# One layer norm for two, later rounding of two batches and ScalarE's own loads, at the start of a gated cross-attention kernel

## The reference

```python
m = jnp.mean(x, axis=axis, keepdims=True)
v = jnp.var(x, axis=axis, keepdims=True)
return (x - m) / jnp.sqrt(v + eps)                     # _layernorm, eps 1e-5
...
return (x - mu) * jax.lax.rsqrt(var + EPS) * w + b     # _ln of the result, EPS 1e-5
...
y = jnp.clip(x.astype(jnp.float32) / scale, -FP8_MAX, FP8_MAX)
y = y.astype(jnp.bfloat16).astype(jnp.float32)
return _fp8_roundtrip(y)                               # _div_clamp_fp8
```

## Time and profile before

| what | value |
|---|---|
| runs | 820.71, 820.9, 822.23 us, median 820.9 |
| the profiled execution's own time | 819.82 us |
| its span in the profile | 818.0 us |
| PE, DVE, ACT, POOL busy | 89%, 75%, 57%, 56% of the span |

### The profile page before, as it was taken

How to read it: one execution, slowest core, us unless ns; L and a number is a source line. 1 busy time by engine, 2 the same in 40 slices (tenths; PEclk the granted TensorE clock), 3 DMA queues, 4 the chain that set the end, 5 groups by cost and what they waited for, 6 DMA issues and landing times.

```text
span 818.0 us, 15329 instructions
## 1 busy us (share of the span) xinstructions
PE 726.0 (89%) x4859; PEld 589.4 (72%) x4859; DVE 613.4 (75%) x1290; ACT 466.6 (57%) x1178; POOL 459.7 (56%) x592
## 2 busy tenths in 40 slices
PE   2548999899999989999998999998886886999996
PEld 2546787778788778878787878887664654777775
DVE  6867888788888878889887898987876592444554
ACT  3656867677676767867667686775652231222221
POOL 3464777566777756777775767776673213222220
PEclk9779999999999999999999999999999596999999
DMA  5320000100010010001001010000020103666661
GB/s 181 97 64 1 27 27 1 52 27 27 1 40 15 1 53 26 26 7 48 1 1 53 1 33 27 1 3 0 1 60 0 64 2 110 191 187 189 199 192 53
DMA packets 44478, 42.74 MB, mean 52 GB/s; under 512 B 3717, under 2 KB 43386, under 8 KB 44410
## 3 DMA queue, kind: packets, MB, share of 16 engines
q1 hardware_dynamic: 42874, 36.62, 14.8%
q0 software_dynamic: 1536, 5.28, 2.4%
HBM read 39.52 MB, written 2.37 MB: 51 GB/s over the span
## 4 chain that ended last, share of the span: by engine, by line
PE 62%; DVE 20%; issue 6%; ACT 5%; POOL 4%; SPq 2%; DMA 1%; POOLq 0%; DVEq 0%; ACTq 0%
PE out_ps L1718 8%; PE proj_ps L1458 7%; PE s_ps L1502 6%; PE proj_ps L1443 5%; PE pT_ps L1511 5%; PE aux_ps L1521 5%; PE aux_ps L1535 5%; DVE q_tok L1086 5%; PE aux_ps L1472 4%; PE proj_ps L1434 4%; PE work_ps L1710 3%; POOL rstd L527 3%; PE work_ps L1732 2%; DVE ss L1066 2%; DVE pT_sb L1111 2%
## 5 line engine op out<-in xcount | busy, mean ns | idle before, releaser
L542 POOL TENSOR_SCALAR p_sb<-p_sb,psum_row 128x256 f32<-128x256 f32 x256 | 125.8, 507 | 69.0 <-DVE psum_row L1105 67.7
L796 ACT ACTIVATE p_sb<-s_ps,negmax 128x256 f32<-128x256 f32 x256 | 118.5, 473 | 66.3 <-DVE negmax L1100 65.2
L1521 PE MATMUL aux_ps<-pT_sb,v_sb 128*128 128x512 f32 x256 | 122.3, 601 | 6.1 <-DVE pT_sb L1111 6.1
L1111 DVE COPY pT_sb<-pT_ps 128x512 f32<-128x512 f32 x128 | 87.7, 686 | 47.5 <-PE pT_ps L1511 46.8
L1502 PE MATMUL s_ps<-kT,qT 128*128 128x256 f32 x768 | 112.7, 289 | 8.2 <-DVE qT L1096 4.6
L549 POOL TENSOR_TENSOR y_bf<-y_bf,mg_bf 128x512 bf16<-128x512 bf16 x64 | 86.0, 1343 | 58.5 <-DVE mg_bf L1123 58.5
L1502 PEld LDWEIGHTS s_ps<-kT,qT 128*128 128x128 f32 x768 | 98.0, 190 | 18.3 <-issue 18.3
L1100 DVE TENSOR_REDUCE negmax<-s_ps 128x2 f32<-128x512 f32 x128 | 86.5, 683 | 5.9 <-PE s_ps L1502 5.6
L527 POOL TENSOR_TENSOR rstd<-var,minus_half 128x8 f32<-128x8 f32 (+1 forms) x64 | 86.6, 1354 | 5.5 <-POOL var L523 0.4
L552 POOL TENSOR_TENSOR catq<-y_bf,mg_bf 128x512 fp32r<-128x512 bf16 x64 | 79.5, 1242 | 5.0
L1535 PE MATMUL aux_ps<-wpT,catq 128*128 128x256 f32 x512 | 71.0, 293 | 7.5 <-DVE wkvT L1017 4.8
(11 more groups left out here) (174 smaller groups left out, 1381.4 us busy)
## 6 DMA issues: line engine op xcount, KB each, us to landing
w_up_a<-in_L_ffn_gate_up_proj SPq DMA_DIRECT2D x16, 384.0 KB, 3.5
w_up_b<-in_L_ffn_gate_up_proj SPq DMA_DIRECT2D x16, 384.0 KB, 3.5
wp_raw<-in_L_xattn_wproj SPq DMA_DIRECT2D x16, 256.0 KB, 2.9
w_down_a<-in_L_ffn_down_proj SPq DMA_DIRECT2D x16, 192.0 KB, 3.5
w_down_b<-in_L_ffn_down_proj SPq DMA_DIRECT2D x16, 192.0 KB, 3.5
w_raw<-in_L_xattn_w_kv_x SPq DMA_DIRECT2D x8, 256.0 KB, 4.0
w_raw<-in_L_xattn_wq SPq DMA_DIRECT2D x7, 256.0 KB, 2.6
w_raw<-in_L_xattn_wqx SPq DMA_DIRECT2D x7, 256.0 KB, 2.9
```

The lines of the kernel that those rows point to most:

```text
L542: ins = nc.gpsimd.tensor_scalar(p_sb[:, r, st, :], p_sb[:, r, st, :], rsum[:, r, st:st + 1], 1.0, ALU.mult, ALU.mult)
L796: ins = nc.scalar.activation(p_sb[:, r, st, :], s_ps[:, r % 2, st, :], ACT.Exp, bias=negmax[:, r, st:st + 1], accum_out=psum_row[:, r, st: ...
L1111: nc.vector.tensor_copy(pT_sb[:, r // 2, r % 2, :, :], pT_ps[:, r % 2, :, :]).then_inc(pT_ready, 1)
L1521: ins = nc.tensor.matmul(aux_ps[:, f.bank, :], v_sb[:, (2 * s.n + tt) % VRING, ty, s.gi, :], pT_sb[:, ty, :, tt, :], start=(tt == 0), stop ...
```

## The change

- The two norms become one: statistics of `x` only, and the variance becomes v (1 + EPS) + EPS². Four batches of statistics, normalisation and POOL's reciprocal root fall away.
- The last 8 small vectors and all 8 scalars are issued by ACT, ahead of its first work, as is a small activation. SP's order becomes two batches of `x`, 7 vectors, the other two batches, k/v weights, context.
- ACT does `ln_out(1)` and `quant_y(1)` before `ctx_hi`, and batch 2 before the first squares. The two tanh of the gates move to sub-step 2.
- DVE rounds batch 1 before the first `sums`. Batch 2 is split around `scaled_kv` and `wq_lo`. The subtraction of batches 2 and 3 moves from POOL to DVE (`quant_less`).
- PE transposes batches 2 and 3 among the weights.

```diff
+        VECTORS = [("L0_xattn_ln_w", 0), ("L0_xattn_ln_b", 2), ("L0_xattn_q_in_scale", 4), ("L0_xattn_k_in_scale", 6),
...
+            load_x(0)
+            load_x(1)
             sp.wait_ge(rows_clear, 1)
...
+            load_vectors(sp, VECTORS[:7])
+            load_x(2)
+            load_x(3)
...
+            load_kv(0, 0)
             sp.dma_start(ctx_raw, t["ctx_2048"].rearrange("b (n p) h -> p (b n) h", p=P)).then_inc(ctx_loaded, 16)
-            load_kv(0, 0)
             load_kv(0, 1)
             load_wq(0, wq0_raw, wq0_loaded)
-            for i, name in enumerate(SCALARS):
-                sp.dma_start(scal[:, i:i + 1], t[name].partition_broadcast(P)).then_inc(scal_loaded, 16)
...
-            for count in range(7):
-                ln_rstd(count)
+            for b in range(NB):
+                ln_rstd(b)
             quant_sub(0)
-            ln_rstd(7)
...
-                if i == 0:
-                    quant_sub(2)
...
-                if i == 0:
-                    quant_sub(3)
...
+            act.wait_ge(rows_clear, 1)
+            load_vectors(act, VECTORS[7:])
+            for i, name in enumerate(SCALARS):
+                act.dma_start(scal[:, i:i + 1], t[name].partition_broadcast(P)).then_inc(scal_loaded, 16)
+            act.wait_ge(memset_done, 3)
+            nc.scalar.activation(gate[:, 3:4], minus_half[:, 0:1], ACT.Identity)
             ln_out(0)
             quant_y(0)
+            ln_out(1)
+            quant_y(1)
...
-            ln_out(1)
-            quant_y(1)
-
-            act.wait_ge(scal_loaded, 16 * len(SCALARS))
-            nc.scalar.activation(gate[:, 0:1], scal[:, 6:7], ACT.Tanh).then_inc(gate_ready, 1)
-            nc.scalar.activation(gate[:, 2:3], scal[:, 7:8], ACT.Tanh).then_inc(gate_ready, 1)
+            ln_out(2)
+            quant_y(2)
...
             squares_kv(0, 0)
+            evac_v(0, 0)
             wq_hi(0, 0)
             wq_hi(1, 0)
-            evac_v(0, 0)
-            ln_out(2)
             ln_out(3)
-            quant_y(2)
...
+                if i == 2:
+                    act.wait_ge(scal_loaded, 16 * len(SCALARS))
...
+                nc.vector.tensor_scalar(mv[:, nt, 1], mv[:, nt, 1], 1.0 + EPS, EPS * EPS, ALU.mult, ALU.add
+                                        ).then_inc(var8_ready, 1)
...
+            def quant_less(b):
+
+                dve.wait_ge(z_ready, b + 1)
+                dve.wait_ge(xq_ready, b)
+                nc.vector.tensor_tensor(xq[:, b, :, :, :].rearrange("p a c k -> p (a c) k"), q_y[b % 2], q_mg[b % 2],
+                                        ALU.subtract).then_inc(xq_ready, 1)
...
+            ln_stats(0)
+            ln_stats(1)
+            ln_norm(0)
             vectors()
...
+            quant_exponents(1)
+            quant_round(1)
             sums(0, 4)
-            quant(1)
+            quant_exponents(2)
             scaled_kv(0, 0)
             wq_lo(0, 0)
             wq_lo(1, 0)
+            quant_round(2)
...
                 if i == 0:
-                    quant(2)
+                    quant_less(2)
...
+                if i == 0:
+                    quant_exponents(3)
+                    quant_round(3)
+                    quant_less(3)
                 if s0:
                     sums(q_seq(s0.a), 8)
-                if i == 0:
-                    quant(3)
...
+            transpose_h(2)
             for c, x in KV_ORDER:
                 fill_kv(c, x, 0)
             for i in range(2, 4):
                 transpose_ctx(i)
+            transpose_h(3)
```

More of the change, by code:

```diff
@@ L383, in qk_parts, with load_vectors, load_x @@
             return qk_f[:, 0, :], [qT[:, part, int(x == "TX"), :, :].rearrange("p a b -> p (a b)") for part in range(2)]
+        VECTORS = [("L0_xattn_ln_w", 0), ("L0_xattn_ln_b", 2), ("L0_xattn_q_in_scale", 4), ("L0_xattn_k_in_scale", 6),
+                   ("L0_xattn_v_in_scale", 8), ("L0_xattn_qx_in_scale", 10), ("L0_xattn_proj_smooth", 20),
+                   ("L0_xattn_qln_w", 12), ("L0_xattn_qln_b", 13), ("L0_xattn_qxln_w", 14), ("L0_xattn_qxln_b", 15),
+                   ("L0_xattn_kln_w", 16), ("L0_xattn_kln_b", 17), ("L0_xattn_kxln_w", 18), ("L0_xattn_kxln_b", 19)]
+        def load_vectors(eng, vectors):
+            for name, row in vectors:
+                n = t[name].shape[0] // P
+                eng.dma_start(vec_rows[row:row + n, :], t[name].rearrange("(r p) -> r p", p=P)).then_inc(vec_loaded, 16)
         @block.sync
         def _(sp):
-            for b in range(NB):
+            def load_x(b):
                 sp.dma_start(x_sb[:, TPB * b:TPB * (b + 1), :], t["x"][b, :, :].rearrange("(n p) h -> p n h", p=P)
                              ).then_inc(x_loaded[b], 16)
+            load_x(0)
+            load_x(1)
             sp.wait_ge(rows_clear, 1)
[L392 to L399, removed]
+            load_vectors(sp, VECTORS[:7])
+            load_x(2)
+            load_x(3)
             def load_rows(dst, name, row, n, done):
@@ L497, in _, with ln_rstd @@
                                         base=0, pattern=[[-1, P]], channel_multiplier=1).then_inc(const_ready, 1)
-            def ln_rstd(count):
-                pool.wait_ge(var8_ready, count + 1)
-                b = LN_STATS[count][1]
+            def ln_rstd(b):
+                pool.wait_ge(var8_ready, b + 1)
                 nt = slice(TPB * b, TPB * (b + 1))
@@ L851, in _ @@
                     quant_y(3)
+                if i == 2:
+                    act.wait_ge(scal_loaded, 16 * len(SCALARS))
+                    nc.scalar.activation(gate[:, 0:1], scal[:, 6:7], ACT.Tanh).then_inc(gate_ready, 1)
+                    nc.scalar.activation(gate[:, 2:3], scal[:, 7:8], ACT.Tanh).then_inc(gate_ready, 1)
                 if s1:
@@ L943, in link, with ln_stats, ln_norm @@
                 dve.wait_ge(dve_chain, chain[0])
-            def ln_step(scale, i, b):
-                src = (x_sb, h_sb)[i]
+            def ln_stats(b):
                 tiles = range(TPB * b, TPB * (b + 1))
[L949 to L955, removed]
-                    if i == 0:
[L957 to L967, removed]
+                dve.wait_ge(x_loaded[b], 16)
+                for n in tiles:
+                    ins = nc.vector.bn_stats(stat[:, n, :], x_sb[:, n, :])
+                link(ins)
+                for n in tiles:
+                    ins = nc.vector.bn_aggr(mv[:, n, :], stat[:, n, :])
+                link(ins)
+                nt = slice(TPB * b, TPB * (b + 1))
+                nc.vector.tensor_scalar(mv[:, nt, 1], mv[:, nt, 1], 1.0 + EPS, EPS * EPS, ALU.mult, ALU.add
+                                        ).then_inc(var8_ready, 1)
+            def ln_norm(b):
+                dve.wait_ge(rstd8_ready, b + 1)
+                for n in range(TPB * b, TPB * (b + 1)):
+                    ins = nc.vector.tensor_scalar(h_sb[:, n, :], x_sb[:, n, :], mv[:, n, 0:1], rs8[:, n:n + 1],
+                                                  ALU.subtract, ALU.mult)
+                ins.then_inc(h_ready, 1)
             def vectors():
@@ L983, in weight_scales, with quant_exponents @@
                 ins.then_inc(wscale_ready, 1)
-            def quant(b):
+            def quant_exponents(b):
                 y, mg = q_y[b % 2], q_mg[b % 2]
@@ L1030, in wq_lo @@
                 ins.then_inc(aux_free[f.bank], 1)
-            for step in LN_STEPS[:7]:
-                ln_step(*step)
+            ln_stats(0)
+            ln_stats(1)
+            ln_norm(0)
             vectors()
-            for step in LN_STEPS[7:12]:
-                ln_step(*step)
+            ln_norm(1)
+            ln_stats(2)
+            ln_stats(3)
+            ln_norm(2)
+            ln_norm(3)
             weight_scales()
-            quant(0)
+            quant_exponents(0)
+            quant_round(0)
             ctx_lo(0)
@@ L1045, in _ @@
             ctx_lo(3)
-            for step in LN_STEPS[12:]:
-                ln_step(*step)
             def wp_lo(ty, g):
@@ L1357, in transpose_h @@
             def transpose_h(b):
-                pe.wait_ge(h_ready, [st[1:] for st in LN_STEPS if st[0]].index((1, b)) + 1)
+                pe.wait_ge(h_ready, b + 1)
                 wait(pe, yT_ready, b - 1)
@@ L1585, in _ @@
             project_kv(0, 0)
-            transpose_h(2)
-            transpose_h(3)
             fill_wq(0, 0)
```

6 lines of the change are left out of this document (2 added, 4 removed).

## The result

The changed kernel takes **815.47 us** in the median of five runs (813.1 to 816.3), against 820.9 before. The ratio is 0.9931 with an interval of 0.9911 to 0.9951, so it is faster by 0.5 to 0.9%, some 5.4 to 5.7 us where 3.9 were forecast. The profiled execution took 813.1 us with a span of 811.3, and was the quickest of the five: two took 813.1 and 813.3 at a mean granted clock of 0.973, three 815.5 to 816.3 at 0.969. Against the profile of before its span is 6.7 us shorter.

A forecast was written before the change was run, and what follows sets the result against it. The start was taken as bound by waits through SP's queue to the last scalar. Terms -3.92 - 0.19 - 0.99 + 0.98 + 0.19 = -3.93 took 819.82 to 815.9, expected median 817.0, range 815.3 to 820.5.

The forecast's parts named there:

- What bounds the start: Start up to `kv_lo`: everything waits for SP's last scalar, issued at 15.42; earlier scalars and reordered work bring `kv_lo` -3.92.
- ACT's loads: Start, ACT's queue: sixteen loads at SP's prices end at 7.73, so `ln_out(0)` starts at 9.2 instead of 12.89.
- The rival of two queues sharing what makes the loads: Start: SP and ACT take turns, ACT's 6.78 us of loads double, sum +2.85, 823.8, slower; chance 0.10.
- The rival of late scalars: Start: scalars wait behind context and weights, land at 19.1 as before, gain nil, 820.9; chance 0.08.
- From `kv_lo` to the squares: `kv_lo` to first squares: list the same length, 10.59; only the two tanh go, -0.19.
- `k_tok` behind `rstd`: First `k_tok`: batch 1 is rounded ahead of `sums`, so `k_tok` follows `rstd` at once, at 33.58: -0.99.
- To the last `wq_lo`: `k_tok` to last `wq_lo`: 11.99 as before, set by PE's projection and ACT's `quant_y(3)`; no change.
- The cover: Before `wq_lo(1, 1)`, due at 44.7: DVE's batch 2 work and `scaled_kv`, about 43.9, fit with little to spare.
- Batch 3 in the open: Last `wq_lo` to `q_tok`: rounding, subtraction, `sums` and POOL's root in sequence, 8.92 instead of 7.94: +0.98.
- The tanh: Sub-step 2, on ACT: the two tanh come back there, +0.19 at most.
- After `q_tok`: Behind first `q_tok`: chain is PE's, `qk_lo`'s vanished 3.64 us counts nothing, everything stays about 4 us earlier.

The follow-up runs named there:

- The loads alone: Kernel before with SP's new load order, ACT's sixteen loads and the small activation, two norms and old rounding kept: 816.32 us, 0.9956.
- the norm alone: Kernel before with the two norms joined as one and nothing else edited: 820.29 us, 1.0004.
- four scalars later: Changed kernel with the last four scalars issued by SP behind the weights instead of by ACT: 814.81 us, 0.9929.
- the run with PE kept busy: Kernel before with 54 unread identity transposes on PE in its wait for the first `kv_lo`: 818.74 us, 0.9984.
- the changed kernel with PE kept busy: Changed kernel with 30, 28 and 54 unread identity transposes in three of PE's waits up to the first queries: 811.47 us, 0.9891.

## Why the prediction was right in direction and short in size

- **What bounds the start: right.** The loads alone gave 0.9956, the norm alone 1.0004. The last scalar is issued at 7.36 where it was at 15.42.
- **ACT's loads: short by 1.2**, 8.89 against 7.73, by the last two, which took 0.79 and 1.53. `kv_lo` was short by 0.95. The run with four scalars later shows that only 0.3 of this was ACT's to give, for the context lands at about 15.4 and PE, ACT and DVE follow it. The run with the subtraction back on POOL agrees: its loads kept the forecast time (7.74), and `kv_lo` came at 20.35. I had not put the context on the path at all.
- **The rival of two queues sharing what makes the loads: seen, but small.** Fourteen of ACT's loads cost 0.21 to 0.52, as on SP; two cost more. The Trainium skill (DMA: Bandwidth & Descriptors, Issuing engines are not separate DMA queues) says that issuing from several engines saves only the sequencer's time, and that the transfers interleave. The trace fits both halves: the last scalar was issued 8 us sooner, but landed only at about 14.4, 7 us after its issue began, where it took 3.68 before. Here the sequencer's time was what counted.
- **The rival of late scalars: nearer than it looked.** They had to land by 15.2, were forecast for 11.4, and landed at about 14.4. DVE's norms, too, ended at 13.84 and not near 12, since the last batch of `x` kept DVE waiting for 1.24. Neither counted: DVE still waited 1.06 for `ctx_hi` before `ctx_lo`.
- **From `kv_lo` to the squares: the failed step.** "The list is the same length: 10.59" was taken from a stretch in which PE's clock was at 0.50 up to 30 us, and I had read no clock there. It took 8.54. Beyond the tanh that is 1.86 less, and the run with PE kept busy took 8.65 with no other edit; the loads alone took 8.64.
- **`k_tok` behind `rstd`: right**, -0.94 for -0.99. **To the last `wq_lo`: right**, -0.02 for nothing. The cover held: `wq_lo` waited for ACT. But there is luck in it. Both kernels have a low granted clock in this stretch, before (first line) and after (second line), so the same unread term happened to cancel:

```profile
40.00:45.00 5.00, 5.00 (x26) 4.42 (x25) 1.77 (x5) 4.02 (x11) 2.93 (x1) 0.66 0.35 109
...
35.00:40.00 5.00, 4.42 (x24) 3.76 (x23) 4.96 (x4) 2.04 (x5) 2.39 (x2) 0.78 0.00 1
```

From `k_tok` both took 11.1. With the clock at 1.00 while PE projects there, it took 10.3 (the kernel before with PE kept busy, and the loads alone) and 10.4 (the changed kernel with PE kept busy).

- **Batch 3 in the open: right.** From the end of `wq_lo` (44.69) to `q_tok` it took 8.92, for a forecast of 8.92.
- **The tanh: right**, +0.21 for +0.19, between the second and third `q_tok`.
- **After `q_tok`: not foreseen.** The first trace won 0.66 more up to the second `q_tok` and 1.5 at 560 us, both with a higher granted clock. The same kernel in another execution did not.

In sum, at `q_tok` -4.12 was forecast. The loads and the context took 0.95 off it, the clock added 1.86, and -5.00 came out (the other steps differ by 0.03). That the two misses have opposite signs, so that the first takes back half of the second, is luck. The medians' 5.4 to 5.7 lie inside what the two traces of the changed kernel allow. What stays open is what makes the low stretch behind `q_tok` longer in one execution than in another. Open too is whether the 2.0 us between the loads alone (816.32) and the whole change (814.36 in its six runs) are real: their intervals overlap, and at the first `q_tok` their traces differ by 0.3 or less.

## What to carry to other kernels

Before a stretch is called "unchanged", read the granted clock in it: a wait that is taken away can also take away the low clock behind it, so that a long preparation shrinks by more than its wait. When small loads gate the start, spread their issue over two queues, and then ask which transfer binds next; here it was the context, and putting the weights ahead of it was worth 2.7 us at `kv_lo` (17.59 against 20.29). An instruction that is quicker on another engine (2.29 for 4.07) still costs if it moves from behind the awaited work to ahead of it.

## What was not expected of the hardware

- A small POOL instruction can wait out a whole DVE instruction: `var`, 128x4, took 2.06 beside DVE's subtraction (39.00 to 41.29), and 0.20 when the subtraction was on POOL. The other way round DVE's 128x2048 instruction took 2.34 instead of 0.69 until POOL's subtraction (32.60, 4.08) was done. The Trainium skill (SBUF — State Buffer, Who interferes with whom) says that a DVE instruction with two inputs in SBUF contends with a POOL instruction that reads SBUF, and that against DVE's two-port modes whoever issues first holds the shared pair of ports for the whole instruction; these rows agree.
- After its idle time up to 15.46 PE ran eight transposes in 1.97, and the same eight at 23.21 in 1.04, though the granted clock reads 1.00 from 15 to 30 us. A restart can be slow where that column shows nothing.
- A load's issue on ACT took up to 1.53 while SP issued two large loads (3.36 for both), against 0.48 otherwise. In the run with the subtraction back on POOL the same two took 0.60 and 0.46 beside the same loads of SP, so what makes them wait is not shown.
